# Four small layers on one core: new queue orders and fillers, and the statistics of x1 off VectorE

## The chip, the cores and the metric

The kernel runs on one core of a Trainium2 chip. The metric is the device time of one execution in microseconds, the median of the timed runs. In the text VectorE is DVE, ScalarE is ACT, GpSimd is POOL and TensorE is PE, as in the rows of the profile.

## What is computed

The input x has 4 images of 128 channels and 16 x 16 positions, float32. Four blocks follow one another, each on the group-normalised sum so far, with 32 groups of 4 channels:

```python
x = x + attention(gn(x))            # layer 0: q, k, v, softmax, output projection, over 256 positions
x = x + binary_conv(gn(x))          # layer 1: batch norm, sign, 3x3 grouped conv with sign weights, batch norm, residual, PReLU
x = x + depthwise_pointwise(gn(x))  # layer 2: depthwise 3x3, norm, relu, prune; pointwise, norm, relu, prune
x = x + linear_attention(gn(x))     # layer 3: softmax over positions of k, context of k and v, times q, output projection
```

The sums after each block are x1, x2, x3 and x4. Channels lie on the 128 partitions, so one image is a tile of 128 x 256. Batch norm in layer 1 needs all four images; the group norms need one image (in layer 2 a pair).

## The kernel before

The program has no loops at run time and no scheduler. Each engine has a block of code in which small functions are defined and then called in an order written out by hand, such as `attend(b)`, `x1_out(b)` or `depthwise(p, tap)`. An engine goes through its own list strictly in order; between engines there are only semaphores, which a function waits for at its head and raises at its end. So a function that waits holds up everything listed behind it on its engine. b is the image, p a pair of images, r and par halves.

Layer 0 on TensorE (L1325 to L1385): `project_q`, `project_k`, `project_v` per image, `scores` (two matmuls into bank 3 or 4), `transpose_prob` (four transposes), `attend` (four matmuls). Into the values the output projection is folded: `fold_weights` and `fold_bias` make `setup` once, and `project_v(0)` needs it. VectorE takes out k (`k_out`), the row maxima (`row_max`), the inverse sums (`rinv_out`) and x1 (`x1_out`, L918), ScalarE q, exp, the transposed probabilities and the values (`v_out`). The outputs of images 0, 1 and 2 lie in bank 6, so `attend(1)` and `attend(2)` wait until x1 of the image before is out.

The statistics of x1: VectorE does `bn_stats` over the tile, `bn_aggr` and a mean square (L789 to L800). TensorE sums them over the channels of a group (`group_means`, L1292, a matmul with 2 columns), VectorE reads that and makes the variance (`group_out`, `group_var`), GpSimd takes the root (`gn_root`, L363), VectorE normalises (`norm1`). Then `bn1_mean_sq`, `bn1_mean`, `bn1_var` on VectorE make the batch norm of layer 1 from the channel and group statistics, GpSimd takes its root, ScalarE makes the signs and TensorE the convolution (`conv`, 36 matmuls, L1394).

GpSimd's list in that time: valid mask, head masks (for layer 3), the roots of images 1 to 3, `x_bias` for four images (needed by `x1_out`), `dw_diagonals` (weights of the depthwise convolution as diagonals of 32 x 32 tiles), constants of layer 2, `conv_weights` (nine products), `sw_root` (scale of the binary weights), and then the roots of layer 1. `sw_scale` on VectorE waits for `sw_root`.

`valid_taps` (L1410) is the depthwise convolution of a tile of ones, nine taps of four matmuls. It lies on TensorE beside the end of layer 0's statistics. `keep_warm(n, bank)` (L1277) issues n bf16 matmuls of 128 x 256 whose result nobody reads: fillers.

Layer 2: a pair p of images has its depthwise convolution in nine taps of eight 32 x 32 matmuls (L1455). The tile of the array that a matmul takes is chosen so that pair 0 and pair 1 take different ones:

```python
side = (r % 2, 1 - r % 2)[p]
at = (2 * i + side) * TILE
```

Group means (`group_means2`) come in between, `less_mean` closes a pair, `relu1` on ScalarE and `prune1_max`, `prune1_weights` on VectorE make the inputs of `pointwise`. Then `prune2_max`, `prune2_floor`, `x3_out` on VectorE, `square_sum3` on ScalarE and `group_means3` on TensorE lead into layer 3, where ScalarE normalises images 0 and 1 (`norm3_first`, L645, with `norm_bias_out` of GpSimd ahead) and VectorE images 2 and 3 (`norm3`). Layer 3 on TensorE: `project_k3`, `project_q3`, `project_v3`, `transpose_k`, `context`, `project_context`, `output`; VectorE's `x4_out` makes the result, which SyncE stores image by image.

## Time and profile before

| what | us |
|---|---|
| timed runs: median of 3, lowest to highest | 76.19 (76.15 to 77.23) |
| the profiled execution | 75.42 |
| its span (first to last instruction) | 73.7 |
| busy in it: TensorE, VectorE, GpSimd, ScalarE | 62.6, 44.6, 31.3, 30.7 |
| the four stores' issues, last x4 on VectorE | from 68.84; until 70.64 |

All times in the rows are counted from the start of the span of that one execution. A row of the timeline merges instructions of one line that follow each other: its second number is the time from the first's start to the last's end. The end of a matmul is modelled and overlaps the next one's start, so the step from one row's start to the next row's start says more than the sum of the lengths. A bracket says how long the engine was idle before the row, and what ended that. Float32 matmuls stand in the rows as two records each.

### The profile page before, as it was taken

The page shows a single profiled execution, that of the slowest core. Times are in us where ns is not written, and L with a number is a line of the kernel's source. Part 1 is how long each engine was busy: PE and PEld are TensorE (multiplying, and loading weights), DVE is VectorE, ACT ScalarE, POOL GpSimd, SP SyncE. Part 2 cuts the span into 40 slices and gives each one's busy share as a digit, 9 for nine tenths or more (in the row PEclk, how much of TensorE's full clock was granted, in tenths as well). Part 3 has the DMA queues.
Part 4 walks back from the last instruction along what each step waited for, and adds up shares of the span by engine and source line. Part 5 has one row for each costly group of instructions (what it writes and reads, how often), then busy time and mean ns, then how long its engine had stood idle before and what let it go on. Part 6 is the DMA issues. An engine that isn't in the chain of part 4 may idle for free.

```text
span 73.7 us, 1931 instructions
## 1 busy us (share of the span) xinstructions
PE 62.6 (85%) x704; PEld 49.0 (67%) x704; DVE 44.6 (60%) x167; ACT 30.7 (42%) x89; POOL 31.3 (42%) x92
## 2 busy tenths in 40 slices
PE   3979999999992999958998899999554999999900
PEld 2645888888991984517886578875142988999600
DVE  3779654467554997888366970065697447635630
ACT  5102031848990510029008780060383848784200
POOL 6706858988895312530002007006448519620000
PEclk9999999999999999999999999999998579999999
DMA  0897210000000000000000000000000000000124
GB/s 2 201 387 160 38 21 0 0 0 0 0 13 0 4 0 0 0 0 9 0 0 0 0 0 9 9 0 9 4 0 0 0 0 0 0 0 0 63 88 147
DMA packets 2778, 2.14 MB, mean 29 GB/s; under 512 B 976, under 2 KB 2512, under 8 KB 2768
## 3 DMA queue, kind: packets, MB, share of 16 engines
q1 hardware_dynamic: 2768, 2.01, 9.5%
q8 instruction: 6, 0.10, 0.5%
q14 instruction: 4, 0.03, 0.1%
HBM read 1.49 MB, written 0.52 MB: 27 GB/s over the span
## 4 chain that ended last, share of the span: by engine, by line
PE 43%; POOL 28%; DVE 13%; issue 9%; ACT 2%; POOLq 0%; ACTq 0%; DVEq 0%
PE bank L1455 7%; PE bank L1394 6%; POOL conv_blocks L394 4%; POOL gn_rstd L363 4%; PE bank L1540 3%; PE bank L1521 3%; PE bank L1531 3%; POOL x_bias L382 3%; PE bank L1586 3%; PE bank L1381 3%; PE bank L1566 2%; PE bank L1296 2%; PE bank L1410 2%; DVE h_linear L1092 2%; POOL bn_rstd L363 2%
## 5 line engine op out<-in xcount | busy, mean ns | idle before, releaser
L363 POOL TENSOR_TENSOR gn_rstd<-gn_var_eps,minus_half 128x1 f32<-128x1 f32 (+2 forms) x12 | 7.4, 620 | 8.3 <-DVE gn_var_eps L812 8.0
L1280 PE MATMUL bank<-warm 128*128 128x256 bf16 x36 | 7.0, 357 | 1.1 <-POOL warm L347 1.1
L1455 PE MATMUL bank<-x,dw_diag 32*32 32x256 f32 x288 | 7.6, 381 | 0.3 <-DVE x L1055 0.3
L1455 PEld LDWEIGHTS bank<-x,dw_diag 32*32 32x32 f32 x288 | 5.2, 103 | 1.6 <-issue 0.9
L1280 PEld LDWEIGHTS bank<-warm 128*128 128x128 bf16 x36 | 4.5, 129 | 2.4 <-POOL warm L347 1.1
L664 ACT ACTIVATE h<-bank,l_shift,dw_scale 128x256 f32<-128x256 f32 x4 | 2.2, 560 | 7.4 <-PE bank L1483 7.1
L1394 PE MATMUL bank<-signs,conv_blocks 128*128 128x256 bf16 x36 | 4.3, 276 | 1.2 <-ACT signs L602 1.2
L1357 PE MATMUL bank<-k,q 128*128 128x256 f32 x16 | 5.0, 444 | 0.0
L602 ACT ACTIVATE signs<-res,bn_shift,bn_scale 128x256 bf16<-128x256 f32 x4 | 2.2, 595 | 6.6 <-DVE bn_shift L996 6.6
L1394 PEld LDWEIGHTS bank<-signs,conv_blocks 128*128 128x128 bf16 x36 | 3.4, 97 | 2.2 <-issue 1.6
L1092 DVE TENSOR_SCALAR_CACHE_REDUCE h_linear<-bank,dw_scale 128x256 f32<-128x256 f32 x4 | 1.9, 480 | 4.6 <-PE bank L1483 4.6
L1410 PE MATMUL bank<-valid,dw_diag 32*32 32x256 f32 x72 | 4.5, 378 | 0.0
L1381 PE MATMUL bank<-vt,probT 128*128 128x128 f32 x32 | 4.4, 280 | 0.0
L363 POOL TENSOR_TENSOR bn_rstd<-bn_var_eps,minus_half 128x1 f32<-128x1 f32 x2 | 1.2, 600 | 7.4 <-DVE bn_var_eps L1012 6.6
L910 DVE TENSOR_REDUCE nmax<-bank 128x2 f32<-128x512 f32 x4 | 2.8, 691 | 2.3 <-PE bank L1357 2.3
L1381 PEld LDWEIGHTS bank<-vt,probT 128*128 128x128 f32 x32 | 3.9, 192 | 0.0
L1296 PEld LDWEIGHTS bank<-gn_mean_sq,group_avg 128*128 128x128 f32 x10 | 1.7, 214 | 3.3 <-DVE gn_mean_sq L798 2.4
L1540 PE MATMUL bank<-late_params,t 128*128 128x128 f32 x16 | 3.1, 322 | 0.9 <-ACT t L648 0.9
L1357 PEld LDWEIGHTS bank<-k,q 128*128 128x128 f32 x16 | 3.4, 228 | 0.5
L581 ACT ACTIVATE prob<-bank,nmax 128x256 f32<-128x256 f32 x8 | 3.7, 475 | 0.0
L790 DVE BATCH_NORM_STATS2 gn_stats<-x 128x6 f32<-128x256 f32 x8 | 3.4, 422 | 0.3 <-DMA x<-in_x 0.2
L1296 PE MATMUL bank<-gn_mean_sq,group_avg 128*128 128x2 f32 x10 | 2.0, 269 | 1.8 <-DVE gn_mean_sq L798 1.8
(186 smaller groups left out, 160.5 us busy)
## 6 DMA issues: line engine op xcount, KB each, us to landing
out<-x SPq DMA_DIRECT2D x4, 128.0 KB, 2.4
late_params<-in_late SPq DMA_DIRECT2D x1, 404.5 KB, 4.9
x<-in_x SPq DMA_DIRECT2D x1, 384.0 KB, 3.6
early_params<-in_early SPq DMA_DIRECT2D x1, 258.0 KB, 3.8
x<-in_x SPq DMA_DIRECT2D x1, 128.0 KB, 2.1
pw_weights<-in_late SPq DMA_DIRECT2D x2, 64.0 KB, 3.8
pw_weights<-in_late SPq DMA_DIRECT2D x4, 32.0 KB, 1.8
l_params<-in_late SPq DMA_DIRECT2D x4, 2.2 KB, 1.7
```

The source lines that it names most:

```text
L363: return nc.gpsimd.tensor_tensor(out_ap, in_ap, minus_half[:, 0:n], ALU.pow)
L581: nc.scalar.activation(prob[:, b, par, :], s_ps[b % 2][:, par * N:(par + 1) * N], ACT.Exp, bias=nmax[:, b, par:par + 1], accum_out=psum_ro ...
L790: step(nc.vector.bn_stats(st[:, layer, b, :], xs[layer][:, b, :]), "stats", layer, b)
L1092: nc.vector.tensor_scalar(h2_linear[:, p, r, :], dw_ps[p][r], dw_scale[:, p, r:r + 1], None, ALU.mult, ALU.max, accum_out=amax1[:, p, r:r ...
L1280: nc.tensor.matmul(bank[:, 0:N], warm[:, 0:C], warm[:, :], start=True, stop=True)
L1296: nc.tensor.matmul(gn_ps[:, 0:2], group_avg[:, :], mv[:, layer, b, 0:3:2], start=True, stop=True).then_inc(group_ready[layer], 1)
L1357: ins = nc.tensor.matmul(s_ps[b % 2][:, par * N:(par + 1) * N], q[:, b, par:N:2], k[:, b, :], start=True, stop=True)
L1381: ins = nc.tensor.matmul(o_ps[b][:, par * C:(par + 1) * C], probT[:, b, j, par, :], vt[:, b, j, :], start=(j == 0), stop=(j == 1))
L1394: ins = nc.tensor.matmul(conv_ps[b], conv_w[:, tap, :], signs[:, b, dy:dy + H, dx:dx + W], start=(tap == 0), stop=(tap == TAPS - 1))
L1410: ins = nc.tensor.matmul(valid_ps[of], dw_diag[of, tap, :], valid[of, dy:dy + H, dx:dx + W], start=(tap == 0), stop=(tap == TAPS - 1))
L1455: nc.tensor.matmul(tile_of(p, i, r), dw_diag[of, tap, :], xs[2][of, 2 * p + i, dy:dy + H, dx:dx + W], start=(tap == 0), stop=False)
L1540: ins = nc.tensor.matmul(vt_ps[:, j * C:(j + 1) * C], t3[:, b, j * C:(j + 1) * C], wqkv[2], start=True, stop=True)
```

## The change

It has five parts.

1. Orders. The lists of all four computing engines are rearranged, from layer 0 to layer 3. In layer 0, `project_k(0)`, `fold_bias` and `project_v(0)` come earlier on TensorE, and `row_max`, `attend` and `transpose_prob` earlier; in layer 2 the taps of pair 0 come first and those of pair 1 after them; in layer 3 values come ahead of keys and outputs ahead of late queries. On VectorE `tile_consts` goes behind the first statistics and `sw_scale` ahead.
2. Statistics of x1. `x1_out` gives out the sum of each half with its accumulator, GpSimd adds the halves (`x1_sums`), ScalarE sums the squares (`x1_square`). `group_means` of layer 1 uses `group_sum`, which has the 1/256 in it. `x1_channel_stats` on GpSimd gives mean and variance per channel to `bn1_mean_sq`. VectorE's `bn_stats`, `bn_aggr` and mean square of x1 are gone.
3. Banks. The output of image 1 has bank 0 (q's) instead of bank 6, so `attend(1)` waits for the last q instead of x1 of image 0, and `attend(2)` for x1 of image 0.
4. Who does what. The values of images 2 and 3 are copied out by VectorE (`v_late_out`), the nine diagonals of the depthwise weights are made one at a time by ScalarE (`dw_diagonal`) instead of at once by GpSimd; the convolution weights on GpSimd come in three portions between the `x_bias` of the images; `sw_root`, the constants of layer 2 come early, head masks and group swaps late. Image 0 of layer 3 is normalised by VectorE, image 1 by ScalarE; the copies of q of layer 3 go to ScalarE but for image 2.
5. Fillers. Ten behind the valid taps ahead of the convolution, and five, four and four around `group_means3(0)` and `(1)`, ahead of `pointwise(1)`.

```diff
-        o_ps = [banks[i][:, 0:N] for i in (6, 6, 6, 1)]
+        o_ps = [banks[i][:, 0:N] for i in (6, 0, 6, 1)]
...
+            def x1_sums(b):
+
+                pool.wait_ge(x1_ready, 2 * b + 2)
+                nc.gpsimd.tensor_tensor(mv[:, 1, b, 0:1], x1_sum[:, b, 0:1], x1_sum[:, b, 1:2],
+                                        ALU.add).then_inc(x1_sum_ready, 1)
...
+                step(nc.gpsimd.tensor_scalar(bn1_m[:, :], mv[:, 1, :, 0], 1.0 / N, 0.0, ALU.mult, ALU.add))
+                nc.gpsimd.tensor_scalar(bn1_e[:, :], mv[:, 1, :, 2], 1.0 / N, 0.0, ALU.mult, ALU.add)
+                step(nc.gpsimd.tensor_tensor(bn1_msq[:, :], bn1_m[:, :], bn1_m[:, :], ALU.mult))
+                nc.gpsimd.tensor_tensor(bn1_v[:, :], bn1_e[:, :], bn1_msq[:, :],
+                                        ALU.subtract).then_inc(x1_channel_ready, 1)
...
+            def dw_diagonal(tap):
...
+                at = LC["dw"].start + tap
+                nc.scalar.activation(dw_diag[:, tap, :], ident_tile[:, :], ACT.Copy,
+                                     scale=lp[:, at:at + 1]).then_inc(dw_diag_ready, 1)
...
+            def x1_square(b):
+
+                act.wait_ge(x1_ready, 2 * b + 2)
+                nc.scalar.activation(squares[:, 0, b, :], xs[1][:, b, :], ACT.Square,
+                                     accum_out=mv[:, 1, b, 2:3]).then_inc(x1_square_ready, 1)
...
                     nc.vector.scalar_tensor_tensor(
                         out=xs[1][:, b, side], in0=o_ps[b][:, side], scalar=rinv[:, b, par:par + 1],
-                        in1=xb[:, b, side], op0=ALU.mult, op1=ALU.add).then_inc(x1_ready, 1)
-
-            def x1_stats(b):
-                dve.wait_ge(x1_ready, 2 * b + 2)
-                gn_stats(1, b)
+                        in1=xb[:, b, side], op0=ALU.mult, op1=ALU.add,
+                        accum_out=x1_sum[:, b, par:par + 1]).then_inc(x1_ready, 1)
+
+            def v_late_out(b):
+                dve.wait_ge(v_mm, b + 1)
+                nc.vector.tensor_copy(vt[:, b, :, :].rearrange("p a c -> p (a c)"),
+                                      v_ps).then_inc(v_late_ready, 1)
...
-                if b == 3:
+                if b == 1:
+                    pe.wait_ge(q_ready, B)
+                elif b == 2:
+                    pe.wait_ge(x1_ready, 2)
+                elif b == 3:
                     pe.wait_ge(k_ready, B)
-                elif b >= 1:
-                    pe.wait_ge(x1_ready, 2 * b)
...
+            keep_warm(5, gap_warm_ps)
             group_means3(0)
+            keep_warm(4, gap_warm_ps)
+            group_means3(1)
+            keep_warm(4, gap_warm_ps)
             pointwise(1)
```

TensorE in the middle of layer 0, before: `t0` and `setup` make the values in bank 2, `ident` transposes the probabilities, `vt` and `probT` are attend, `gn_mean_sq` the group means.

```order
L1357 MATMUL bank4<-k,q 128x256 x2
L1368 MATMUL bank5<-ident,prob 128x128 x4
L1381 MATMUL bank6<-vt,probT 128x128 x4
L1368 MATMUL bank5<-ident,prob 128x128 x4
L1345 MATMUL bank2<-setup,t0 128x128 x2
L1381 MATMUL bank6<-vt,probT 128x128 x4
L1296 MATMUL bank7<-gn_mean_sq,group_avg 128x2
L1345 MATMUL bank2<-setup,t0 128x128 x2
L1368 MATMUL bank5<-ident,prob 128x128 x4
L1381 MATMUL bank6<-vt,probT 128x128 x4
L1296 MATMUL bank7<-gn_mean_sq,group_avg 128x2
L1381 MATMUL bank1<-vt,probT 128x128 x4
```

The same stretch now, from attend(0) on:

```order
L1436 MATMUL bank6<-vt,probT 128x128 x4
L1418 MATMUL bank5<-ident,prob 128x128 x4
L1407 MATMUL bank4<-k,q 128x256 x2
L1395 MATMUL bank2<-setup,t0 128x128 x2
L1418 MATMUL bank5<-ident,prob 128x128 x4
L1436 MATMUL bank0<-vt,probT 128x128 x4
L1395 MATMUL bank2<-setup,t0 128x128 x2
L1344 MATMUL bank7<-gn_mean_sq,group_sum 128x2
L1418 MATMUL bank5<-ident,prob 128x128 x4
L1436 MATMUL bank6<-vt,probT 128x128 x4
L1344 MATMUL bank7<-gn_mean_sq,group_sum 128x2
L1436 MATMUL bank1<-vt,probT 128x128 x4
```

The last scores (bank 4) stood ahead of attend(0) and now stand behind it, both value projections stand ahead of the first group means, and attend(1) writes bank 0.

GpSimd between the constants of layer 2 and the roots of layer 1, before: `conv_blocks` are the convolution weights, `sw_rstd` the scale's root, `gn_rstd` the four roots of layer 1.

```order
L382 TENSOR_TENSOR x_bias<-x0,setup 128x256 x4
L440 TENSOR_TENSOR dw_diag<-ident_tile,late_params 128x288
L408 TENSOR_SCALAR l2_var_eps<-l2_params 128x5
...
L394 TENSOR_TENSOR conv_blocks<-conv_sign,conv_mask 128x128 x9
L363 TENSOR_TENSOR sw_rstd<-sw_var,minus_half 128x1
L363 TENSOR_TENSOR gn_rstd<-gn_var_eps,minus_half 128x1 x4
```

And now; `gn_mean_sq<-x1_half_sum` is x1_sums:

```order
L391 TENSOR_TENSOR x_bias<-x0,setup 128x256
L406 TENSOR_TENSOR conv_blocks<-conv_sign,conv_mask 128x128 x3
L415 TENSOR_TENSOR gn_mean_sq<-x1_half_sum 128x1
L391 TENSOR_TENSOR x_bias<-x0,setup 128x256
L406 TENSOR_TENSOR conv_blocks<-conv_sign,conv_mask 128x128 x3
L391 TENSOR_TENSOR x_bias<-x0,setup 128x256
L415 TENSOR_TENSOR gn_mean_sq<-x1_half_sum 128x1
L372 TENSOR_TENSOR gn_rstd<-gn_var_eps,minus_half 128x1
L415 TENSOR_TENSOR gn_mean_sq<-x1_half_sum 128x1
```

The root of sw has left this stretch for the front, and the first x1_sums now stands ahead of x_bias of images 2 and 3 and three weight products.

TensorE in layer 2, before, from the tap behind the first group means on: banks 3 and 4 are pair 0, banks 0 and 1 pair 1, `valid_sum` is less_mean.

```order
L1455 MATMUL bank3<-x2,dw_diag 32x256 x4
L1455 MATMUL bank4<-x2,dw_diag 32x256 x4
L1455 MATMUL bank0<-x2,dw_diag 32x256 x4
L1455 MATMUL bank1<-x2,dw_diag 32x256 x4
...
L1483 MATMUL bank3<-valid_sum,mean_diag 32x256 x4
```

And now, from the closing of pair 0 to pointwise(1), taps of one pair in a row shown once:

```order
L1538 MATMUL bank4<-valid_sum,mean_diag 32x256 x4
L1510 MATMUL bank0<-x2,dw_diag 32x256 x4
...
L1562 MATMUL bank2<-h2,pw_kept 128x256
L1510 MATMUL bank0<-x2,dw_diag 32x256 x4
...
L1538 MATMUL bank1<-valid_sum,mean_diag 32x256 x4
L1323 MATMUL bank5<-warm 128x256 x5
L1548 MATMUL bank7<-gn_mean_sq,group_sum 128x2
L1323 MATMUL bank5<-warm 128x256 x4
L1548 MATMUL bank7<-gn_mean_sq,group_sum 128x2
L1323 MATMUL bank5<-warm 128x256 x4
L1562 MATMUL bank3<-h2,pw_kept 128x256
```

Before, ten taps alternated between the pairs (five of each) and seven taps of pair 1 stood ahead of pointwise(0); now all of pair 1 comes behind less_mean(0), six of its taps behind pointwise(0).

## Rows read from the trace of the kernel before

**Rows 1.** The page: busy time, granted clock in 40 slices, the chain by engine.
```profile
PE 62.6 (85%) x704; PEld 49.0 (67%) x704; DVE 44.6 (60%) x167; ACT 30.7 (42%) x89; POOL 31.3 (42%) x92
...
PEclk9999999999999999999999999999998579999999
...
PE 43%; POOL 28%; DVE 13%; issue 9%; ACT 2%; POOLq 0%; ACTq 0%; DVEq 0%
```

**Rows 2.** Timeline of TensorE, 7.5 to 17 us: start, length, line, what, idle before.
```profile
8.98 1.06 PE L1335 MATMUL bank<-t,early_params 128*128 128x256 f32 x2
9.83 0.64 PE L1309 MATMUL bank<-early_params,bias_rows 128*128 128x128 f32 x2
...
10.70 1.85 PE L1357 MATMUL bank<-k,q 128*128 128x256 f32 x4
12.39 0.61 PE L1345 MATMUL bank<-setup,t 128*128 128x128 f32 x4
...
16.77 1.03 PE L1357 MATMUL bank<-k,q 128*128 128x256 f32 x4
```

**Rows 3.** Timeline of TensorE, end of layer 0 to the convolution.
```profile
21.30 1.13 PE L1381 MATMUL bank<-vt,probT 128*128 128x128 f32 x8
23.77 0.38 PE L1296 MATMUL bank<-gn_mean_sq,group_avg 128*128 128x2 f32 x2 [1.35 <-DVE gn_mean_sq L798]
...
26.02 1.14 PE L1381 MATMUL bank<-vt,probT 128*128 128x128 f32 x8
...
27.31 1.06 PE L1410 MATMUL bank<-valid,dw_diag 32*32 32x256 f32 x16
...
29.18 0.38 PE L1296 MATMUL bank<-gn_mean_sq,group_avg 128*128 128x2 f32 x2
...
33.47 4.26 PE L1394 MATMUL bank<-signs,conv_blocks 128*128 128x256 bf16 x36 [1.18 <-ACT signs L602]
```

**Rows 4.** Timeline of GpSimd, 19 to 24 us.
```profile
19.35 3.25 POOL L394 TENSOR_TENSOR conv_blocks<-conv_sign,conv_mask 128x128 bf16<-128x128 bf16 x9
22.56 0.57 POOL L363 TENSOR_TENSOR sw_rstd<-sw_var,minus_half 128x1 f32<-128x1 f32 x1
```

**Rows 5.** Timeline of VectorE, 23 to 28 us.
```profile
23.16 0.21 DVE L889 TENSOR_SCALAR sw<-sw_abs_sum,sw_rstd 128x1 f32<-128x1 f32 x1 [1.55 <-POOL sw_rstd L363]
...
27.95 0.42 DVE L790 BATCH_NORM_STATS2 gn_stats<-x 128x6 f32<-128x256 f32 x1
```

**Rows 6.** Timeline; windows of L1455: length, matmul and load busy (records), clock, DMA.
```profile
41.95 1.53 PE L1455 MATMUL bank<-x,dw_diag 32*32 32x256 f32 x48 [0.33 <-DVE x L1055]
...
50.87 1.09 PE L1455 MATMUL bank<-x,dw_diag 32*32 32x256 f32 x32
...
45.10:46.10 1.00, 1.00 (x78) 0.88 (x64) 1.00 0.00 0
50.87:51.90 1.03, 1.03 (x32) 0.47 (x32) 1.00 0.06 16
```

**Rows 7.** Timeline; a window: PE, loads, DVE, ACT, POOL busy, then granted clock.
```profile
52.14 0.67 PE L1483 MATMUL bank<-valid_sum,mean_diag 32*32 32x256 f32 x16 [0.18 <-POOL mean_diag L456]
...
54.60 1.14 PE L1507 MATMUL bank<-h,pw_kept 64*128 64x256 f32 x8 [0.27 <-ACT h L664]
...
56.97 1.22 PE L1540 MATMUL bank<-late_params,t 128*128 128x128 f32 x4 [0.93 <-ACT t L648]
...
59.70 0.42 PE L1493 MATMUL bank<-gn_mean_sq,group_sum 128*128 128x2 f32 x2
...
58.00:59.00 1.00, 1.00 (x4) 0.82 (x4) 0.07 (x2) 0.82 (x3) 0.27 (x1) 0.50 0.00 0
```

**Rows 8.** Timeline of VectorE: a read of the accumulator, and the last outputs.
```profile
41.72 0.08 DVE L1055 DVE_READ_ACCUMULATOR x<-h_neg,one_minus_a,bank 128x1 f32 x1
41.72 0.48 DVE L1037 SCALAR_TENSOR_TENSOR h<-bank,bn_scale,res 128x256 f32<-128x256 f32 x1
...
69.67 0.97 DVE L1150 SCALAR_TENSOR_TENSOR x<-bank,out_bias,x 128x256 f32<-128x256 f32 x2 [0.42 <-PE bank L1586]
```

276 lines of the change are left out of this document (151 added, 125 removed).

## Prediction

> **What bounds the kernel now.** I read the page first: TensorE (PE in the rows) is busy 85% of the 73.7 us span, yet only 43% of the chain that ended last is TensorE's; GpSimd (POOL) has 28% of it [rows 1]. So no engine is simply full: the kernel is one long chain in which TensorE works nearly all the time and loses time in a few places. The granted clock shows one of them: it is full but for three slices around 55 to 60 us [rows 1]. Then I read TensorE's timeline for those places. There are three.
>
> First, the start. Until about 12.4 us a projection or score pass costs about twice what it costs later: the two score matmuls of image 0 last 1.85 us from 10.70, those of image 2, at 16.77, 1.03 [rows 2]. The page prints a full clock there [rows 1], but the first durations are those of the 1.2 GHz level.
>
> Second, the end of the attention of layer 0. TensorE's attend(1) starts at 21.30, and before 23.77 it sits idle for 1.35 us, waiting for the statistics of x1 of image 0 [rows 3]. VectorE made these late, because it stood 1.55 us at sw, in its queue ahead of them, waiting for GpSimd's sw_rstd [rows 5]; and GpSimd did that root only at 22.56, behind nine conv_blocks products of 3.25 us [rows 4]. Behind group_means(1, 0) in TensorE's queue stand project_v(3), transpose_prob(3), attend(2), attend(3), and all of them moved with it.
>
> Third, the way into layer 3. project_v3(0) waits 0.93 us for ScalarE's t and starts at 56.97; by then the clock has been halved, and it, the keys and the queries of image 0 last until 59.70 [rows 7]. From there TensorE has work until the last output.
>
> **Layer 0, start.** project_k(0) moves ahead of other_group_means. It can start when t of image 0 is ready, near 7.1, instead of waiting in line until 8.98 [rows 2]. Its 0.9 us are used; other_group_means slips by as much, but GpSimd no longer has the head masks ahead of its root, so the other three images are normalised no later. fold_bias starts near 8.5 instead of 9.83, setup comes back on ScalarE near 9.95, and project_v(0) goes before scores(0). Then q(0) at 9.4, v(0) at 10.2, scores(0) at about 11.1. With the clock coming up at the same moment as before, scores(0) ends near 12.5, with the values already done; before, both were done at about 12.84 (scores to 12.39, and a value pass of 0.45 at the full clock). I take -0.3 us. ScalarE's nine dw_diag products (about 0.2 each, the small activations' price, my estimate) lie in its idle time there: 0.7 us in the worst case, if q waited for all of the seven ahead of it; zero in the best. I take zero, since q(0) itself is what comes later.
>
> **Layer 0, attention.** The row maxima go first on VectorE, transpose_prob(0) stands ahead of scores(1), attend(0) ahead of scores(3), and o_ps of image 1 has bank 0, so attend(1) no longer waits for x1 of image 0. The statistics leave VectorE: four times the stats of 0.42 [rows 5] with an aggregation and a mean square, about 2.8 us by my estimate; in their place come two copies of values (about 0.4 each), one square sum per image on ScalarE (about 0.5) and one tiny sum on GpSimd. GpSimd does sw_rstd right after the other roots, near 10 us, so the 1.55 us at sw go. What is late next? On GpSimd, x1_sums(0) now waits for x1 of image 0 with x_bias(2), (3) and three conv products queued behind it. With attend(0) now near 17.7, x1(0) comes near 19.4, so the block behind it, some 2.6 us, is done near 22.1, and x1_sums(1) is wanted only after x1(1), near 22.6. That has 0.5 us of slack and is the tightest place of the new order.
>
> TensorE's queue from q(1) to the end of attend(3) was 12.84 to 27.16 (26.02 plus 1.14), 14.3 us with 1.35 idle [rows 3]. Without the idle time and with 0.3 to 0.5 of small gaps closed, it ends at 12.5 + 12.6 = 25.1, so -2.0. Part of that is given back: group_means(1, 3) now stands behind four valid taps and the scale row, 1.0 (16 records, two taps) + 0.3 + 0.3 + 1.0 = 2.6 after attend(3), at 27.7 to 27.8, against 29.18 before [rows 3]: -1.4. From there the chain through VectorE, GpSimd and the signs is as long as before (norm1(2) takes norm1(1)'s place in it), 4.3 us to the convolution, so it starts near 32.05 instead of 33.47 [rows 3]. The channel statistics on GpSimd (four small operations, 0.9) are done near 27.4, a microsecond before VectorE asks. The ten fillers end near 31.2 and cost nothing. **Term A: -1.4 us** (bounds: -0.6, if GpSimd or the new order of TensorE makes one new wait of 0.8; -2.1, if nothing is given back).
>
> A second reading of the same edit: x1_out now gives out its sum. The Trainium skill ("VectorE: DVE Perf Modes", on two Vector instructions with no wait between them) says that an operation that also writes its accumulator is two instructions. By that rule alone the eight halves would cost eight reads of 0.08, 0.65 us. The trace has such reads already: the one at 41.72 starts together with the next operation, so none holds the queue [rows 8], and the sum has nothing for it.
>
> **Convolution to x2.** No edit that matters; all of it moves by term A. I keep the old times of the trace below, to compare.
>
> **Depthwise convolution.** This edit costs time. A tap is 16 records. Where taps of one pair follow each other, 3 take 1.53 us and 2 take 1.09, so each further tap costs 0.44; where taps of pair 0 and 1 alternate, 78 records pass in 1 us, 0.21 a tap [rows 6]. The pairs use different tiles of the array and run beside each other. The new order does pair 0 first and pair 1 behind it. On the old clock: five taps to 44.3, group_means2(0), four taps to 46.7, mean_diag near 47.0, less_mean(0), relu1 near 47.8 (before: about 48.2); depthwise(1, 0), group_means2(1) near 47.8, two taps, pointwise(0) near 49.5 to 50.3, six taps to 53.0. less_mean(1) starts near 52.85 instead of 52.14 [rows 7]: +0.7. The floors and x3 of images 0 and 1 are made meanwhile, as before. Then five, four and four fillers with group_means3(0) and (1) among them (1.4 us) stand before pointwise(1): it starts near 55.45 instead of 54.60 [rows 7], +0.85.
>
> The Trainium skill ("TensorEngine Tiling (Array Packing)", Key Properties) has it that tiles work independently and that different ones run in parallel; that speaks against this order. Were nothing else to hide it, ten alternating taps at 0.44 in place of 0.21 would cost 2.3 us. The chain of waits says that only part counts, since mean_diag was waited for before (0.18 us, by less_mean(1) [rows 7]).
>
> **Into layer 3.** What starts project_v3(0) is not pointwise(1) but t of image 0. VectorE makes it now, straight from the root: group_means3(0) near 54.0, then its read and variance on VectorE (0.2 each, behind a product in its queue), the root near 55.1 to 55.7, norm3(0) 55.85 to 56.3, project_v3(0) near 56.4. That is -0.55 against 56.97: norm_bias and ScalarE's operation are off the path. With TensorE busy from 50.3 (fillers, then pointwise(1)), the clock should stay up: v, q, k of image 0 take 3 x 0.43 = 1.3 us instead of 2.73 and end near 57.8 instead of 59.70. **Term B: -1.9 us**, of which 1.4 is clock (bounds: -0.4 if the clock falls as before, -2.2).
>
> **Tail.** Before: 59.70 to 70.1, of which nearly all is TensorE's work, with the last x4 pair on VectorE at 69.67 plus 0.97 [rows 8]. The new order's work at the full clock is 9.8 us by the same durations. I find two new waits: group_means3(3) and context(0) stand where the squares of image 3 and the freed bank come 0.5 to 0.7 late, and the last output waits 0.3 for q3 and proj of image 3. 57.8 + 9.8 + 0.95 = 68.55 instead of 70.1. **Term C: +0.35 us** (bounds: -0.5 to +1.3).
>
> **Sum.** -1.4 - 1.9 + 0.35 = -2.95, rounded to -3.0. The profiled execution took 75.42 us; 72.4 is its successor. The median of the timed runs, 76.19, lies 0.77 above it, so I forecast 73.2 us.
>
> **Rivals.** *The clock falls anyway.* The fillers are few (13, about 1.4 us) and the stretch still waits on VectorE. For: the old stretch with gaps fell at 56.6 and came back only after 59.7 [rows 1, 7]. Against: the new one has no gap over 0.3 us that I can find. Price 1.4: 74.6. *The GpSimd queue.* The 0.5 us of slack at x1_sums(1) is not there, or another wait in the reordered attention and tail takes the stall's place: half of term A and all of term C's upper bound, about +1.6, so 74.8, within 2% of before. *The clock comes up earlier.* TensorE has work without a break from about 7 us. If it rose before q(0) and not at the end of scores(0), then q, v and scores of image 0, 3.4 us at the low level (0.85 + 0.85 + 1.7), would cost 1.7 less, of which the chain can use perhaps 1.4: 71.8. *Slower than before.* The depthwise stage now keeps 8 of 16 tiles busy for its whole length. If the clock were halved for that, each of 18 taps would cost 0.44 more; from the seventh tap on the gain of 3.0 is gone, and with all 18 the time is 73.2 + 7.9 = 81.1. Against: the two taps at 50.87, also one pair alone, ran at a granted clock of 1.00 [rows 6]. For: nothing but that such a stretch was never longer than some taps.
>
> **Chances.** Forecast 0.48 (own range 72.3 to 74.2), clock falls 0.15, a new queue wait 0.17, clock earlier 0.12, depthwise at half clock 0.03, others 0.05. A measurement of this kernel can tell about 2%, 1.5 us, from no change. Faster by over that means under 74.67: the forecast, the earlier clock, and a little over half of the two middle rivals: 0.80. Within 2%: 0.14. Slower: 0.06. The range 71.6 to 75.2 leaves two in ten out.
>
> **What would show it.** The wait of VectorE for sw_rstd and TensorE's 1.35 us at group_means are gone; attend(3) ends near 25.1; the convolution starts near 32; the depthwise stage, from its first tap to less_mean(1), is longer by about 0.7; the granted clock has no 0.50 after 50 us; project_v3(0) starts near 55.0 in the new trace (56.4 less term A). It is wrong if GpSimd's x_bias(2) comes after attend(2) has ended, if conv starts after 32.9, if the clock row shows 0.50 in the depthwise or layer 3 stretch, or if the tail from k3(0) on takes over 12 us.

## The result, and the profile after

| | before | after |
|---|---|---|
| timed runs, median (lowest to highest) | 76.17 (76.01 to 77.23), 4 runs | 70.44 (70.33 to 70.64), 4 runs |
| the profiled execution, and its span | 75.42, 73.7 | 70.44, 68.7 |

The ratio of the medians is 0.926, interval 0.923 to 0.929: faster by 5.7 us. I had forecast 73.2 (71.6 to 75.2). The sign was right, the size was not, and the measured time lies below the range.

The page after, against [rows 1]: busy time, granted clock in 40 slices, the chain by engine.

```profile
PE 61.9 (90%) x727; PEld 47.6 (69%) x727; DVE 42.9 (62%) x165; ACT 33.3 (49%) x104; POOL 32.3 (47%) x98
...
PEclk9999999999999999999999999999999999999999
...
PE 66%; issue 10%; DVE 6%; DMA 5%; POOL 4%; ACT 4%; SPq 1%
```

GpSimd was 28% of the chain and is 4%; TensorE was 43% and is 66%. The dip of the clock at 55 to 60 us is gone.

TensorE's timeline after, the same places as [rows 2, 3, 7] (start, length, what, idle before):

```profile
8.19 0.60 PE L1376 MATMUL bank<-t,early_params 128*128 128x256 f32 x2
8.92 0.68 PE L1395 MATMUL bank<-setup,t 128*128 128x128 f32 x4
9.82 1.14 PE L1407 MATMUL bank<-k,q 128*128 128x256 f32 x4 [0.22 <-ACT q L608]
10.79 0.38 PE L1376 MATMUL bank<-t,early_params 128*128 128x256 f32 x1
...
20.45 0.28 PE L1344 MATMUL bank<-gn_mean_sq,group_sum 128*128 128x2 f32 x2
20.72 0.65 PE L1418 MATMUL bank<-ident,prob 128*128 128x128 f32 x4
...
22.25 1.14 PE L1436 MATMUL bank<-vt,probT 128*128 128x128 f32 x8
...
25.84 0.38 PE L1344 MATMUL bank<-gn_mean_sq,group_sum 128*128 128x2 f32 x2
...
30.13 1.07 PE L1449 MATMUL bank<-signs,conv_blocks 128*128 128x256 bf16 x8 [0.41 <-ACT signs L641]
```

Read the scores of image 0 first: 1.14 us where they took 1.85. They now take what later images always took, so the clock is already up, and project_q(1) starts at 10.79 instead of 12.84. Then the means of image 0, at 20.45: no bracket, where 1.35 us of idle time stood. The root they had waited for is now the third root in GpSimd's list, at 9.60 instead of 22.56 [rows 4], and VectorE's sw has no wait [rows 5]:

```profile
9.60 0.54 POOL L372 TENSOR_TENSOR sw_rstd<-sw_var,minus_half 128x1 f32<-128x1 f32 x1
...
13.60 0.20 DVE L939 TENSOR_SCALAR sw<-sw_abs_sum,sw_rstd 128x1 f32<-128x1 f32 x1
```

The depthwise stage and the way into layer 3, against [rows 6, 7]:

```profile
38.62 2.39 PE L1510 MATMUL bank<-x,dw_diag 32*32 32x256 f32 x80 [0.33 <-DVE x L1108]
...
43.90 0.45 PE L1538 MATMUL bank<-valid_sum,mean_diag 32*32 32x256 f32 x8 [0.35 <-POOL mean_diag L475]
...
47.41 2.82 PE L1510 MATMUL bank<-x,dw_diag 32*32 32x256 f32 x96
50.03 0.64 PE L1538 MATMUL bank<-valid_sum,mean_diag 32*32 32x256 f32 x16
...
52.52 1.14 PE L1562 MATMUL bank<-h,pw_kept 64*128 64x256 f32 x8
53.59 0.71 PE L1595 MATMUL bank<-late_params,t 128*128 128x128 f32 x4
54.14 0.60 PE L1586 MATMUL bank<-t,late_params 128*128 128x256 f32 x2
54.57 1.03 PE L1576 MATMUL bank<-t,late_params 128*128 128x256 f32 x4
```

VectorE's normalised x3 of image 0, for which project_v3(0) waits, is done at 53.27:

```profile
52.86 0.41 DVE L871 TENSOR_SCALAR t<-x,gn_mean_floor,gn_rstd 128x256 f32<-128x256 f32 x1
```

Six taps of one pair take 2.62 us, 0.44 each, as forecast. v, q and k of image 0 stand 0.43 to 0.55 us apart, where they had taken 2.73 together at the low level.

The reads of the accumulator at x1 are there, eight of 0.08 or 0.09 us, and cost the queue nothing: the one at 20.60 starts together with the next operation, as the prediction had it.

One more place counts, and I had not looked at it ahead: SyncE, which issues the four stores. Before: the second and the third issue, by two windows of its timeline, and then, of the DMA view of 69.3 to 69.4 us, the instruction queue (packets begun there, MB, their time as a share of 16 engines):

```profile
69.27 1.66 SPq L323 DMA_DIRECT2D out<-x  x1
...
70.97 0.43 SPq L323 DMA_DIRECT2D out<-x  x1
```

```profile
q8 instruction: 1, 0.02, 78.5%
```

After, the last issue:

```profile
66.59 0.33 SPq L332 DMA_DIRECT2D out<-x  x1
```

An issue takes 0.33 to 0.45 us, but one took 1.66. A 16 KB packet of instructions began in that window and lasted 1.26 us (0.785 x 0.1 us x 16), until 70.57. From the end of the last x4 (70.64; after: 66.56) the span went on for 3.05 us before and for 2.15 after.

Where the time went, profile to profile, in the stretches of the prediction:

| stretch | before | after | change | forecast |
|---|---|---|---|---|
| start to project_q(1) | 12.84 | 10.79 | -2.05 | -0.3 |
| to conv(0) | 20.63 | 19.34 | -1.29 | -1.1 |
| to pointwise(1) | 21.13 | 22.39 | +1.26 | +0.85 |
| to project_v3(0) | 2.37 | 1.07 | -1.30 | -1.4 |
| v, q, k of image 0 | 2.73 | 1.41 | -1.32 | -1.4 |
| to the end of the last x4 | 10.94 | 11.56 | +0.62 | +0.35 |
| to the end of the span | 3.05 | 2.15 | -0.90 | 0 |

The miss is 2.76 us. Two rows, the start and the very end, went 2.65 us beyond the forecast, and the other five took 0.67 of that back. The remaining 0.77 us is what I added for the distance of profile and median: the changed kernel's profiled execution is its median. The row of the start compares one execution with one; the next section shows that it varies between executions of one kernel.

### The profile page after: what moved, and what is told of

It is laid out like the page before. It is cut to its first block, busy times and chain, and to the rows that moved or that the text cites. A ratio compares the mean times of both kernels' runs of the same rounds, so it can differ in the third digit from the quotient of the medians.

```text
span 68.7 us, 2001 instructions
## 1 busy us (share of the span) xinstructions
PE 61.9 (90%) x727; PEld 47.6 (69%) x727; DVE 42.9 (62%) x165; ACT 33.3 (49%) x104; POOL 32.3 (47%) x98
## 4 chain that ended last, share of the span: by engine, by line
PE 66%; issue 10%; DVE 6%; DMA 5%; POOL 4%; ACT 4%; SPq 1%
PE bank L1510 9%; PE bank L1449 6%; PE bank L1407 5%; PE bank L1436 5%; DMA x<-in_x 5%; PE bank L1562 3%; PE bank L1621 3%; PE bank L1383 3%; PE bank L1641 3%; PE bank L1595 3%; PE bank L1418 3%; PE bank L1586 3%; PE bank L1576 3%; PE bank L1323 2%; PE bank L1395 2%
## 5 line engine op out<-in xcount | busy, mean ns | idle before, releaser
L1323 PE MATMUL bank<-warm 128*128 128x256 bf16 x59 | 9.7, 316 | 1.1 <-POOL warm L356 1.1
L1510 PE MATMUL bank<-x,dw_diag 32*32 32x256 f32 x288 | 8.9, 376 | 0.3 <-DVE x L1108 0.3
L1323 PEld LDWEIGHTS bank<-warm 128*128 128x128 bf16 x59 | 6.5, 118 | 3.4 <-POOL warm L356 1.1
L1407 PE MATMUL bank<-k,q 128*128 128x256 f32 x16 | 4.2, 387 | 0.2 <-ACT q L608 0.2
L483 POOL TENSOR_TENSOR gn_mean_squared<-gn_group 128x2 f32<-128x2 f32 x2 | 0.5, 240 | 8.3 <-DVE gn_group L1128 8.3
L680 ACT ACTIVATE squares<-x,floor 128x256 f32<-128x256 f32 x4 | 2.0, 507 | 3.2 <-DVE x L1175 3.1
L406 POOL TENSOR_TENSOR conv_blocks<-conv_sign,conv_mask 128x128 bf16<-128x128 bf16 x9 | 3.4, 404 | 0.1
L1407 PEld LDWEIGHTS bank<-k,q 128*128 128x128 f32 x16 | 2.9, 197 | 0.6 <-ACT q L608 0.4
L515 POOL TENSOR_TENSOR rinv<-sum,minus_one 128x1 f32<-128x1 f32 x4 | 2.2, 551 | 2.2 <-ACT e L709 2.2
```

Of the source, the lines that this page charges most:

```text
L406: ins = nc.gpsimd.tensor_tensor(conv_w[:, tap, :].rearrange("p (g o) -> p g o", o=CONV_GROUP), conv_sign[:, tap, :].unsqueeze(1).to_broadc ...
L515: nc.gpsimd.tensor_tensor(rinv3[:, b:b + 1], sum3[:, b:b + 1], minus_one[:, :], ALU.pow).then_inc(rinv3_ready, 1)
L1323: nc.tensor.matmul(bank[:, 0:N], warm[:, 0:C], warm[:, :], start=True, stop=True)
L1407: ins = nc.tensor.matmul(s_ps[b % 2][:, par * N:(par + 1) * N], q[:, b, par:N:2], k[:, b, :], start=True, stop=True)
L1510: nc.tensor.matmul(tile_of(p, i, r), dw_diag[of, tap, :], xs[2][of, 2 * p + i, dy:dy + H, dx:dx + W], start=(tap == 0), stop=False)
```

## The experiments

Three questions: is it the clock that gave 2.05 us at the start, and what set it; what was each moved piece worth by itself; and what made the end shorter. On the chips of the four sets of runs the kernel before had medians of 76.46 (with e1 to e4), 76.45 (c1, e5 to e7), 75.88 (e8 to e11) and 75.94 (e12, e13, c2); its executions spread over 4 us (73.99 to 78.12).

### The start

**e1_before_stats_first**: the kernel before, with one call moved on VectorE.

```diff
-            tile_consts()
             dve.wait_ge(x_in[0], 16)
             gn_stats(0, 0)
             gn_aggr(0, 0)
             gn_mean_sq(0, 0)
+            tile_consts()
```

> The kernel before with one edit: VectorE takes the statistics of image 0 ahead of tile_consts, so TensorE has no idle time of 0.45 us at its first group means. Theory A (this small gap is what kept the clock low until 12.2 us): the granted clock is full before 6 us, q, k, bias and scores of image 0 run at the high level, attention starts about 1.5 us earlier, but the stall at sw_rstd grows by as much of it, since GpSimd's work is not moved; so 75.0 to 75.9 us, and the trace shows L1328 at 0.6 us a pair and not 1.2. Rival B (it is the whole new order of TensorE from 6 to 10 us that raises the clock): clock and times as before, 76.0 to 76.2.

75.11 (73.89 to 75.71, 4 runs), no clear difference from before. In the profile the scores of image 0 started at 9.73, 1 us earlier, and then the windows show the granted clock at half from 8.2 us on:

```profile
6.00:8.00 2.00, 1.01 (x7) 0.70 (x6) 1.69 (x12) 0.26 (x1) 1.94 (x6) 1.00 0.35 53
8.20:10.00 1.80, 1.80 (x8) 1.53 (x7) 1.00 (x5) 0.52 (x2) 1.66 (x4) 0.50 0.18 31
10.00:11.40 1.40, 1.40 (x4) 1.12 (x4) 1.34 (x3) 0.33 (x1) 1.02 (x3) 0.50 0.10 16
12.00:14.00 2.00, 2.00 (x14) 1.71 (x13) 1.10 (x3) 1.76 (x7) 1.92 (x3) 1.00 0.00 0
```

The clock had come up and fell again, after a stretch (6 to 8 us) in which TensorE was busy for only 1.01 of 2.00 us (second number). So it was not enough to come up early. But that idle time is not shown to be the cause of the fall. In e3, below, the start of the kernel before is untouched, TensorE was busy for even less of the same stretch, and the clock stayed up:

```profile
6.00:8.00 2.00, 0.81 (x7) 0.53 (x5) 1.72 (x11) 0.26 (x1) 1.89 (x5) 1.00 0.35 52
```

In e8, with the same start, it was 0.97 us, and the clock stayed up too.

**e2_after_tile_first**: the same edit backwards in the changed kernel.

> The changed kernel with tile_consts back ahead of the first statistics. Theory A: the clock comes up late, near 9 to 12 us, and the time is 1.3 to 1.9 us longer than the changed kernel, about 72.0. Rival B: the clock still comes up at about 5 us, and the time grows by at most the 0.3 us by which the first statistics start later, 70.5 to 70.8.

71.47 (71.39 to 72.72), 1.0 above the changed kernel. project_q(1) at 11.85. TensorE idles ahead of its first group mean as it did before, and the first key pass (two records) takes 1.22 us, where 0.60 is usual later:

```profile
4.78 0.56 PE L1344 MATMUL bank<-gn_mean_sq,group_avg 128*128 128x2 f32 x2 [0.47 <-DVE gn_mean_sq L848]
...
7.28 1.22 PE L1383 MATMUL bank<-t,early_params 128*128 128x256 f32 x2
```

Three of the four executions lie at 71.4 to 71.5, where 14 of 16 of the changed kernel lie at 70.3 to 70.7. This statement's place on VectorE carries about half of the start's gain (1.06 of 2.05 us in the profiles).

**e7_after_old_start**: the changed kernel with the old order of layer 0's start (project_q(0) and project_k(0) behind the other group means, scores(0) ahead of project_v(0), setup_out behind q_out(0)), but with the early statistics.

> The changed kernel with the old order of the start on TensorE (other_group_means, project_q(0), project_k(0), fold_bias, scores(0), project_v(0)) and the matching old order of k_out(0) and setup_out; the statistics still go ahead of tile_consts. Theory A (the new order keeps TensorE from idling near 7 us, where the clock would fall again, as in the first experiment at 8.1): the clock falls for a stretch before 12 us in most executions and the time is about 1.0 to 1.4 longer, 71.4 to 71.9. Rival B (early statistics alone do it, and the order of the start is worth nothing else): within 0.3 us of the changed kernel.

70.36 (70.26 to 71.66) against 70.47 for the changed kernel on the same chip, and project_q(1) at 10.63. The new order of the projections, which I had worked out step by step, is worth nothing measurable.

**c1_after_again** and **c2_after_again**: the changed kernel itself, beside the others.

> The changed kernel itself once more, beside the others of this call, for the moment at which the clock comes up over more executions. Theory (its start keeps TensorE busy without a break from 1.2 to 6.2 us, so the clock comes up early nearly always): nearly all executions at 70.3 to 70.7. Rival (the early clock of the profiled execution was chance): a third or more of them at 71.4 or above.

> The changed kernel itself, as the measure for the other two on this chip: 70.3 to 70.6 in most executions, one in six 1.2 to 1.4 us longer with the clock coming up late.

70.47 (70.27 to 71.85) and 70.66 (70.58 to 71.92). The profiled execution of c2 took 71.92; its trace shows what the long ones have:

```profile
8.00:10.00 2.00, 2.00 (x9) 1.87 (x8) 1.45 (x8) 0.85 (x5) 1.02 (x4) 0.50 0.23 40
10.00:11.00 1.00, 1.00 (x5) 0.64 (x4) 0.49 (x3) 1.00 (x5) 1.00 (x2) 0.50 0.14 24
12.00:14.00 2.00, 2.00 (x13) 1.70 (x12) 1.36 (x3) 1.10 (x4) 1.61 (x7) 1.00 0.00 0
```

One program, two executions: project_q(1) at 10.79 and at 12.27, times 70.44 and 71.92. Not all of the 1.48 us is clock: 0.58 of it was there before the first key pass, since the input landed later. VectorE's statistics of the other images waited for x until 5.42 instead of 4.83, its t of image 0 stands behind them, and TensorE waited for early_params for 1.03 us:

```profile
6.16 0.49 PE L1351 MATMUL bank<-early_params 128*128 128x128 f32 x2 [1.03 <-DMA early_params<-in_early]
...
7.57 0.98 PE L1383 MATMUL bank<-t,early_params 128*128 128x256 f32 x2 [0.70 <-DVE t L871]
```

From the first key pass to project_q(1) it then took 4.70 us instead of 3.80: 0.90 is clock. Whether the late input also made the clock fall is not shown. Of 16 timed executions of this kernel two were of the long kind. The kernel before has q(1) at 12.84 in its profile, and at 10.86 and 10.98 in those of e3 and e8 below, which have the same start and in which the clock was up from the first projections on. So the clock alone is worth 1.98 of the 2.05 us, and the same start can have it early or late.

The Trainium skill ("TensorE: Matmul & The Clock Gate", Part 1) says that the number of slow matmuls at the start differs between runs of one kernel; the traces agree (0.90 us of clock between the two q(1) above, 1.98 between the kernel before and e3). It also puts the cost of the start below 1% of a typical span and advises not to fit to a count of them; here it is those 0.9 to 2.0 us of a span of 69 to 74, and the kernels differ in how often they pay it.

### The moved work of layer 0

**e3_before_sw_root_early**: the kernel before, with one root moved on GpSimd.

```diff
             other_roots()
+            sw_root()
             x_bias(0)
...
             conv_weights()
-            sw_root()
```

> The kernel before with one edit: GpSimd takes sw_root right after other_roots, ahead of x_bias. Theory: VectorE's wait of 1.55 us at sw and TensorE's idle 1.35 us at the first group means of layer 1 are gone, and the time falls by 1.0 to 1.4 us to about 75. Rival (the conv weights or the statistics on VectorE end the wait instead, since GpSimd is as full): less than 0.4 us.

73.57 (72.61 to 74.71), ratio to before 0.976 (0.961 to 0.991). The idle time ahead of the first group means of layer 1 is gone:

```profile
19.61 1.13 PE L1381 MATMUL bank<-vt,probT 128*128 128x128 f32 x8
20.64 0.38 PE L1296 MATMUL bank<-gn_mean_sq,group_avg 128*128 128x2 f32 x2
```

project_q(1) to conv(0) took 19.70 us, against 20.63 before and 19.34 with all of the change. So one moved call makes 0.93 of the 1.29 us; the statistics of x1 on ScalarE and GpSimd, the two banks, the row maxima and the late values share 0.36. The median fell by more, 2.9 us, and the profiled execution by 1.94. But that execution was 1.98 us ahead at project_q(1), before the moved root counts: its clock came up early by chance. And it lost 1.09 us behind project_v3(0), where the half clock lasted longer. The stretch tells what the edit is worth, the time does not.

**e4_after_taps_laced**, and once more on the chip of c2, **e13_after_laced_again**: the changed kernel with the taps of the two pairs alternating as before.

```diff
             depthwise(0, 2)
+            group_means2(0)
             depthwise(0, 3)
             depthwise(0, 4)
-            group_means2(0)
-            depthwise(0, 5)
...
             depthwise(1, 0)
+            depthwise(0, 5)
             depthwise(1, 1)
+            depthwise(0, 6)
...
```

> The changed kernel with the old order of TensorE in the depthwise stage (taps of pair 0 and 1 alternating, group means after three taps). Theory A (taps of one pair in a row cost 0.44 us against 0.21, and that is on the path): less_mean(1) comes 1.2 us earlier relative to the first tap, and the time is 0.8 to 1.2 us below the changed kernel, about 69.4. Rival B (norm3(0) on VectorE and the fillers hold project_v3(0) anyway): no change, 70.3 to 70.6. Rival C: the gap in the stage grows and the clock falls, slower by up to 1.4.

> The changed kernel with the taps of the depthwise laced as before, once more, on one chip with the changed kernel itself. Theory: 0.5 to 0.7 us under it in the executions whose clock comes up early, 69.8 to 70.0 against 70.45, since less_mean(1) and pointwise(1) come 1.3 and 0.7 us earlier. Rival: the median is the same (within 0.2 us), because the stretch ahead of pointwise(1) now idles longer and the clock falls in some executions.

70.14 (69.77 to 71.44, 4 runs) and 70.06 (69.58 to 72.33, 6 runs), the latter beside 70.66 for the changed kernel. less_mean(1) came 1.27 us earlier behind the first tap, pointwise(1) 0.7. It is the fastest version measured, 0.6 us by the medians, with the intervals of the two ratios overlapping (0.926 to 0.946 and 0.940 to 0.954). Without the long executions of either, 69.58 to 70.26 (four) stand against 70.58 to 70.69 (five). With the earlier pointwise(1) of both traces, the order of the taps is a loss inside the change. What is late next is VectorE (e13):

```profile
48.85 0.67 PE L1538 MATMUL bank<-valid_sum,mean_diag 32*32 32x256 f32 x16
...
51.91 1.18 PE L1562 MATMUL bank<-h,pw_kept 64*128 64x256 f32 x8 [0.23 <-DVE h_linear L1145]
```

### The fillers

**e5_after_no_gap_fillers**: the changed kernel without the 13 fillers (5, 4, 4) between less_mean(1) and pointwise(1).

> The changed kernel without the 13 fillers around group_means3(0) and (1); the ten ahead of the convolution stay. Theory A (they hold the clock): the granted clock is halved somewhere between 52 and 56 us, v, q, k of image 0 of layer 3 take the double, and the time is 1.0 to 1.8 us longer, 71.6 to 72.2. Rival B (the new order alone leaves no gap long enough; the fillers only stand in the way of group_means3 and pointwise(1)): same or up to 0.4 us faster, 70.0 to 70.5.

70.42 (70.12 to 71.27) beside 70.47. TensorE now idled 0.53 and 0.36 us there, and the clock stayed at 1.00:

```profile
51.71 0.35 PE L1548 MATMUL bank<-gn_mean_sq,group_sum 128*128 128x2 f32 x2 [0.53 <-DVE gn_group L855]
52.42 1.22 PE L1562 MATMUL bank<-h,pw_kept 64*128 64x256 f32 x8 [0.36 <-DVE h_linear L1145]
```

```profile
52.00:54.00 2.00, 1.64 (x12) 1.09 (x12) 1.60 (x8) 0.17 (x1) 1.57 (x4) 1.00 0.00 0
```

The 1.3 us at v, q and k of image 0 are clock, but with the new order of layer 3 the clock holds without fillers: the old one has three gaps within 4.2 us, 0.27 and 0.93 us [rows 7] and, ahead of them, this one:

```profile
53.94 0.38 PE L1493 MATMUL bank<-gn_mean_sq,group_sum 128*128 128x2 f32 x2 [1.13 <-ACT squares L641]
```

VectorE's norm3(0) has taken the last one away. Which of the three gaps made the clock fall no run separates.

**e11_after_laced_no_gap_fillers**: both edits together.

> The changed kernel with the taps of the depthwise laced as before (less_mean(1) 1.27 us earlier behind the first tap in the run with that edit, pointwise(1) 0.7), and without the 13 fillers around group_means3. Theory: pointwise(1) no longer waits in TensorE's queue behind the fillers, the clock holds as it did without them, 69.7 to 70.0, 0.5 to 0.8 under the changed kernel (70.45). Rival 1: with the gap now longer (the means wait for ScalarE's squares all the same) the clock falls behind pointwise(1), and it takes 1.3 us more: 71.1. Rival 2: the last load of instructions, now 26 instructions later, meets the last stores: 70.5.

69.72 at best, but 71.55 by the median and up to 74.57. The profiled one took 72.72, and its trace puts the excess at the start: project_q(1) only at 13.22, 2.43 us late, with x again landing late (the other images' statistics at 5.49). Behind it, TensorE idled 0.63, 0.34 and 0.68 us in the stretch without fillers, and the clock stayed at 1.00. A store's issue was held as well (below; 0.32 us more at the end). Without the two it would be 70.0, as the theory had it. So this trace gives the 13 fillers no use; whether they keep the clock up in other executions is not shown. (The 74.57 has no trace.)

### The end

**e6_after_output0_late**: does the early first store make the end short? output(0) and x4_out(0) are put back to the end.

```diff
             transpose_k(2)
-            output(0)
...
             project_q3(3)
+            output(0)
             output(1)
```

> The changed kernel with output(0) put back directly ahead of output(1) on TensorE, and x4_out(0) directly ahead of x4_out(1) on VectorE. Theory A (the early store of image 0 takes it out of the crowd at the end; before, 3.05 us passed from the end of the last x4 to the end of the span, now 2.14): the last x4 ends within 0.3 us of where it does now, but the time from there to the end of the span grows by 0.4 to 0.9 us, so 70.8 to 71.3. Rival B (the length of the last store is its own and varies by chance): no change beyond 0.2.

71.15 (70.68 to 73.54). All four stores were issued between 66.23 and 68.39, and still 2.16 us from the last x4 to the end. A crowd of stores is not the cause: the time lies in the range of Theory A, but not through the end. The early output(0) is worth about 0.5 us by itself.

**e8_before_late_fillers**: the kernel before with 18 fillers (36 instructions) on TensorE, in its idle places of 1 us. It was made to tell two things apart that a filler does: it keeps TensorE busy, and it moves all later instructions, and with them the load of instructions.

```diff
             less_mean(1)
+            keep_warm(8, vt_warm_ps)
             group_means3(0)
+            keep_warm(2, vt_warm_ps)
             pointwise(1)
             group_means3(1)
+            keep_warm(8, vt_warm_ps)
             project_v3(0)
```

> The kernel before, with 18 pairs of instructions more on TensorE, all filler products in its idle stretches around group_means3(0), pointwise(1) and project_v3(0): 8, 2 and 8. Theory C (clock): the granted clock no longer falls behind pointwise(1), so v, q and k of image 0 take some 1.3 us less and the last x4 comes 1.2 to 1.4 us earlier. Theory L (instruction load): one issue of a store on SyncE took 1.66 us (69.27 to 70.93) while a 16 KB packet of the instruction queue was under way (69.31 to 70.57), and the issue ended 0.36 us behind it. 36 instructions more on TensorE bring that load some 2 us earlier in the program, ahead of the first store, so every issue takes 0.33 to 0.43 us and from the end of the last x4 to the end of the span it takes 2.15 us instead of 2.9 to 3.4. Both together: about 2.2 us under before (74.2 at 76.4). Rival 1, clock alone (the long end belongs to the old order of layer 3): tail stays at 3.0, 75.1. Rival 2, neither (the clock falls through the order, not through idle time): 76.4, and fillers only delay: 76.8.

73.59 (71.79 to 75.13) against 75.88. (The profiled one is the 71.79, with project_q(1) at 10.98: its start was early by chance.) v, q and k of image 0 start 0.43 to 0.55 us apart, at a clock of 1.00, and the four issues are plain:

```profile
55.70 0.71 PE L1541 MATMUL bank<-late_params,t 128*128 128x128 f32 x4
56.25 0.60 PE L1522 MATMUL bank<-t,late_params 128*128 128x256 f32 x2
56.68 0.59 PE L1532 MATMUL bank<-t,late_params 128*128 128x256 f32 x2
...
66.10 2.16 SPq L324 DMA_DIRECT2D out<-x  x4
```

The load now began at 64.5, ahead of the first store; 2.16 us from the last x4 to the end. Both halves of the expectation came out.

**e10_after_no_fillers**: the other way round, the changed kernel without any of its 23 new fillers, so that the load comes later, among the stores.

> The changed kernel without any of its 23 new filler products (10 ahead of conv(0), 13 around group_means3). Without the last 13 it had run as fast as with them. Theory L (instruction load): 46 instructions fewer on TensorE put the last 16 KB load of instructions about where it was in the kernel before, 0.8 us ahead of TensorE's end, that is between 64.5 and 66.5, where three stores are issued: one issue takes 1.2 to 1.7 us instead of 0.33 to 0.36, and from the last x4 to the end of the span it takes 2.6 to 3.1 us instead of 2.15; 70.9 to 71.4 against 70.45. Rival 1 (the long end belonged to the old order): tail 2.15, and 70.45. Rival 2 (the ten fillers hold the clock ahead of the convolution): granted clock 0.5 somewhere from 28.5 to 33, conv later by up to 1 us, 71 to 72 with a tail of 2.15.

71.06 (70.30 to 73.39). The last issue, and the instruction queue in the window 65.9 to 66.1:

```profile
66.31 1.48 SPq L332 DMA_DIRECT2D out<-x  x1
```

```profile
q8 instruction: 1, 0.02, 44.8%
```

The load lasts 1.43 us (0.448 x 0.2 x 16) from 66.00, the issue ends at 67.79, 0.36 behind it, and the end takes 3.32 us instead of 2.15. That is what the theory asked for. Two of the other five took 70.30 and 70.36, as little as the changed kernel, so the load does not cost this in every execution. Ahead of the convolution TensorE now idles for 1.61 us, and the clock held all the same in this execution:

```profile
30.06 1.18 PE L1449 MATMUL bank<-signs,conv_blocks 128*128 128x256 bf16 x9 [1.61 <-ACT signs L641]
```

All five kernels in which a load and a second store met, by the trace's times:

| kernel | load | held issue | issue's end behind the load's | last x4 to the end |
|---|---|---|---|---|
| before | 69.31 to 70.57 | 69.27 to 70.93 | 0.36 | 3.05 |
| e1 | 69.71 to 71.25 | 70.02 to 71.61 | 0.36 | 3.43 |
| e3 | 67.51 to 68.64 | 67.47 to 69.01 | 0.37 | 2.93 |
| e10 | 66.00 to 67.43 | 66.31 to 67.79 | 0.36 | 3.32 |
| e11 | 67.24 to 68.37 | 67.82 to 68.74 | 0.37 | 2.47 |

In the other twelve profiled executions no issue was longer than 0.43 us. In three of them (after, e4, c2) the load was under way when the *first* store was issued, and in e13 it began during that issue (61.15 to 61.52, the load from about 61.45); none was held. All five held issues began less than 0.8 us after the store before, so it may be that the store before must still be under way on the DMA engine that carries the load. That was not tried.

### How much of the change this is

**e9_before_fillers_stats**: the kernel before with e8's fillers, three more behind the first 14, and e1's moved call. Nothing of the moved work.

> The kernel before with the fillers of the run before this one, three fillers more behind the first 14, and VectorE's statistics of image 0 ahead of tile_consts: nothing of layer 0, of the rows' maxima, of the banks or of layer 3's order is changed. Theory (clock and load): the clock is up by 5 to 7 us in most executions, project_q(1) starts at 10.8 to 11.0 instead of 12.84, the late clock stays, the store's stall is gone: 2.0 + 1.3 + 0.9 = 4.2 us under before, 72.2 at 76.4; what is then left to the changed kernel, 1.5 to 2 us, is what its moved work is worth. Rival (the moved work is worth more than half): 74 or above, with q(1) at 12 or later or the clock at half again from 8 us, as in the run of before with its statistics first (75.11).

71.83 (71.73 to 72.81) against 75.88: 4.05 us by the medians. The best execution of e8, on the same chip and with the old start, was as fast (71.79), and its project_q(1) as early (10.98 against 11.01). What the earlier statistics and the three fillers change is how often it goes well: five of six lie at 71.7 to 72.0 here, one of six there. Now the sw_root wait is the one left:

```profile
20.34 1.13 PE L1382 MATMUL bank<-vt,probT 128*128 128x128 f32 x8
22.53 0.38 PE L1297 MATMUL bank<-gn_mean_sq,group_avg 128*128 128x2 f32 x2 [1.07 <-DVE gn_mean_sq L799]
...
18.09 3.27 POOL L395 TENSOR_TENSOR conv_blocks<-conv_sign,conv_mask 128x128 bf16<-128x128 bf16 x9
21.32 0.57 POOL L364 TENSOR_TENSOR sw_rstd<-sw_var,minus_half 128x1 f32<-128x1 f32 x1
```

q(1) came 1.83 us earlier, the root only 1.24 (22.56 to 21.32): GpSimd's list doesn't run by TensorE's clock, so part of the start's gain was lost at this wait.

**e12_e9_with_sw_root_early**: and e3's moved root.

> The kernel before with 21 fillers, the statistics of image 0 first (the run e9: 71.83, q(1) to conv(0) 21.2 us in its profile) and, new, sw_root ahead of x_bias(0) on GpSimd. Theory (sw_root alone pays for nearly all that the moved work of layer 0 gains): the idle stretch in front of group_means(1, 0) goes, q(1) to conv(0) takes 19.7 us as in the run of before with that edit, instead of 21.2, and the time is 70.3 to 70.9, as fast as the changed kernel (70.45). Rival 1 (the statistics by ScalarE and GpSimd, the banks and the maxima matter too): no better than 71.3. Rival 2 (a transfer of the late store or the clock falls otherwise): q(1) to conv(0) 19.7 but 71.8 or more.

70.40 (70.08 to 71.34), beside 70.66 for the changed kernel. Its profile against the others:

| start of | before | e9 | e12 | after |
|---|---|---|---|---|
| project_q(1) | 12.84 | 11.01 | 10.79 | 10.79 |
| conv(0) | 33.47 | 32.22 | 30.48 | 30.13 |
| pointwise(1) | 54.60 | 53.37 | 51.63 | 52.52 |
| project_v3(0) | 56.97 | 55.75 | 54.00 | 53.59 |
| last x4, end | 70.64 | 67.95 | 66.20 | 66.56 |
| end of the span | 73.69 | 70.09 | 68.36 | 68.71 |

Twenty-one fillers and two moved calls do what the whole change does. Its other parts cancel out: 0.35 gained up to the convolution and about 1.3 from pointwise(1) to project_v3(0), 1.24 lost in the depthwise stage and 0.77 behind project_v3(0) (12.97 us to the last x4 instead of 12.20).

## Why the prediction was wrong

1. **Start: the step that failed.** "With the clock coming up at the same moment as before" gave -0.3; measured -2.05, of which 1.98 is clock (e3 against the kernel before, one start, q(1) at 10.86 and 12.84). The rival *The clock comes up earlier* is what happened. It got 0.12, and its 1.4 us, added to 0.3, is close to the size. My reading failed where I took the moment for a property of the chip: it differs between executions of one start by as much (before, e3 and e8), and the place of one VectorE statement moves it by 1.0 us (e2). That my profile of the kernel before was one with a late clock is partly luck of the draw, though its medians of 75.9 to 76.5 against 74.0 at best suggest that the late ones are the usual ones. What makes the clock come up or fall stays open: TensorE's idle time, the theory of e1, doesn't order the traces (e1 against e3). The rest of that step, the order of the projections, was worth 0 (e7).
2. **End: a term that was missing.** -0.9 us. The row was there: 128 KB stores with 2.4 us to landing and four issues over 3.06 us, where four issues without a stall take 2.16 (e8). I treated the stretch behind the last x4 as fixed. The fillers I priced at nothing moved the load of instructions out of the later stores' way (e8, e10).
3. **The offset.** I added 0.77 us, since the old median lay above the old profile. The old kernel's executions vary by 4 us, at least in part with the clock's moment; the changed kernel's agree within 0.4 us in most cases, and the offset goes. A single execution of each says nothing of such an offset.
4. **Attention: right.** -1.29 against -1.1; the removed wait for sw_rstd is the mechanism, and 0.93 of it by itself (e3). The 0.5 us of slack that I feared at x1_sums(1) held: TensorE has no bracket from 10.79 to the 0.41 at the convolution.
5. **Depthwise stage: right mechanism, size too small.** +0.7 forecast at less_mean(1), +1.22 measured behind the first tap, and e4 takes 1.27 back. The taps cost what I said. Of the 0.5 us on top, 0.2 is there at less_mean(0), behind mean_diag's wait of 0.35, and 0.25 more comes at pointwise(0), which takes 1.06 us where I had 0.8. The rival with half the clock in this stage didn't happen.
6. **Into layer 3: right time, partly for a wrong reason.** -2.62 against -2.8. I credited the fillers with holding the clock. e5 shows that it holds without them, and in e5 project_v3(0) starts just as early, at 53.58. I also said that it would not be pointwise(1) that starts project_v3(0); after the change it is: t was ready at 53.27 and TensorE's queue reached it at 53.59.
7. **Tail: right sign.** +0.62 against +0.35.

## What to carry to other kernels

When TensorE's first passes take twice what the same passes take later, price them as a term of their own, and take more than one profile: here two executions of one start differed by 2 us. Twenty-one fillers and the earliest statistics gave more here than all reordered work. Read the queue engine to the last row: an issue several times as long as its neighbours is a stall, and the instruction load beside it can be moved with a few instructions more or less on the engine that it serves. Before keeping a large reordering, run its one or two cheapest pieces alone.

## What the runs showed that was not expected

A load of 16 KB of instructions can hold a store's issue on another engine's queue: five times, each issue ending 0.36 to 0.37 us behind the load. The Trainium skill ("Runtime: NRT & Kernel Launch", Instruction fetch mechanics) has blocks of this size fetched ahead by the sequencer and the cost mostly hidden. The packet's size agrees; for the fetching engine no run here shows a wait either, but the stores of another engine paid 0.6 to 1.3 us. And that the same load leaves a first store's issue alone (0.37 us at 61.72, with a load from 61.64 on) remains unexplained.

The clock can come up, fall and come up again within the first 12 us (e1, c2). One program has two times 1.4 to 1.5 us apart (c1, c2); in c2, 0.90 of it is clock and 0.58 the input that landed later. Executions of 73.4 to 74.6 us in e6, e10 and e11 have no trace and stay unexplained.
